# Two-layer graph kernel on one core: last row group in two pairs, its variance from parts, and y parts as upper halves of float32 words

## Chip, cores, metric

One core of one Trainium2 chip. The metric is device time in microseconds (us) of the whole kernel; the time before is the median of 3 runs.

## What is computed

The input is x (2048 x 64, float32), a 0/1 matrix adj (2048 x 2048, float32, about two ones per row), and the weights of two layers. Cut to what matters:

```python
# layer 0: exponentially weighted neighbours by rank, at most 100 per row
support = x @ w0
mask = (adj != 0); rank = cumsum(mask, axis=1); deg = rank[:, -1:]
k = minimum(deg, 100); pos = rank - (deg - k)
w = mask * where(pos > 0, 0.5 ** (k - pos), 0)
x = layernorm(x + w @ support + b0)              # eps 1e-5, over 64
# layer 1: mean of the neighbours and the row itself, then row-normalised
deg = clip(sum(adj, axis=1) + 1, 1)
h = (adj @ x + x) / deg
z = concatenate([x, h], axis=1) @ W1 + b1
r = relu(z); r = r / maximum(norm(r, axis=1), 1e-12)
out = layernorm(x + r)
```

## The kernel before, in words

Rows are cut into 16 tiles of 128 partitions, and four tiles make a group (0 to 3). The order of work on each engine is written out by hand: every engine has its own program, in order, and semaphores tie them. The adjacency matrix comes in 1 MB pieces, TensorE transposes it (`transpose_adj`, L648; it reads the upper bf16 halves of the float32 words as stationary operand) into `adjT`, VectorE copies it out of PSUM (L484), and for each tile of columns TensorE counts ranks (`count`, L662 and L664, into PSUM `cnt`), ScalarE turns the counts into bf16 weights (`weights`, L296), and TensorE multiplies them with the support (`weigh`, L675, into `acc`). A count waits for the weights of the count before it in its chain. Chain 0 (groups 0 and 2) and chain 1 (groups 1 and 3, five ticks behind) alternate in one loop of 37 ticks (L742 to L770).

VectorE finishes layer 0 of each group (`finish_layer0`, L405 to L439), giving `x1`. TensorE transposes it (`transpose_x1`, L685) and multiplies with W1 (`multiply_x1`, L694) to y and u. y is kept as three bf16 parts in `ysp` beside a column of ones: ScalarE rounds the first part (`y_high`, L307), VectorE subtracts (L431), ScalarE rounds the second (`y_middle`, L312), VectorE subtracts again for the third (L438, semaphore `y_ready`). `aggregate` (L706) multiplies the transposed adjacency (with the identity added, L248 on GpSimd) with these 193 columns, 16 source blocks for each of 16 row tiles, 256 matmuls; they are called in portions as blocks become ready: `early` is blocks 0 to 7, `third` 8 to 11, `fourth` 12 to 15 (L739 to L741, L765 to L797). Group 0 sums in the lower half of `acc`, group 1 in the two `cnt` banks, group 2 in the upper half of `acc`, group 3 in `tmp`. Semaphore `agg_done` counts finished groups.

Behind it stands the end of the kernel, for each group k of four tiles. VectorE: `clip` (degree, L503), `total` (sum of the three parts, L506), `limit` (L511). ScalarE: `weigh_u` (u times degree, four activations, L346). VectorE: `add_u` (L517). ScalarE: `relu` (L351). VectorE: `norm_stats` (two batch-norm statistics, L388), `mean_square` (L527), `add_spread` (L532), `clamp` (L538). GpSimd: `norm_power` (power -0.5, L252). Then r is centred and scaled: for groups 0 and 1 by VectorE's `shift_mean` (L543) and four ScalarE activations (`shift_scale`, L356), for groups 2 and 3 on VectorE (`centre` L548, `scale` L554). VectorE: `add_x1` (L559), `spread_stats` (L388 again). GpSimd: `spread_power` (multiply and add, L256, then power -0.5, L259). VectorE: `output` (L568). SyncE stores each group (L216), in the order 1, 0, 2, 3. The list of calls that sets VectorE's order stands in L571 to L620, GpSimd's in L262 to L269, ScalarE's in L359 to L368. VectorE's own dependencies go through the semaphore `chain` (`done`, `need`).

Of the kernel before, what the change touches and what calls it, by code (L numbers as in the profile page):

```python
# [33 lines left out]
STORES = (1, 0, 2, 3)  # L34
# [9 lines left out]
def build(nc, x, adj, w0, b0, w1, b1, out):  # L44
    with ExitStack() as ctx:  # L45
# [22 lines left out]
        ysp = sb("ysp", [P, NB, PD + 2], BF16)  # L68
# [11 lines left out]
        stats = sb("stats", [P, 2, NB, 3], F32)  # L80
# [3 lines left out]
        shift = sb("shift", [P, NB], F32)  # L84
        power = sb("power", [P, RT], F32)
        eps = sb("eps", [P, 1], F32)
        root = sb("root", [P, 2, NB], F32)
        small = sb("small", [P, 4, NB], F32)
# [40 lines left out]
        y_mid = sem("y_mid")  # L129
# [4 lines left out]
        degree_ready = [sem(f"degree_ready{k}") for k in range(Q)]  # L134
        weighted = [sem(f"weighted{k}") for k in range(Q)]
        z_ready = [sem(f"z_ready{k}") for k in range(Q)]
        relued = [sem(f"relued{k}") for k in range(Q)]
        clamped = [sem(f"clamped{k}") for k in range(Q)]
        norm_root = [sem(f"norm_root{k}") for k in range(Q)]
        shift_ready = [sem(f"shift_ready{k}") for k in range(Q)]  # L140
        scaled = [sem(f"scaled{k}") for k in range(Q)]
        spread_ready = [sem(f"spread_ready{k}") for k in range(Q)]
        spread_root = [sem(f"spread_root{k}") for k in range(Q)]
        power_set = sem("power_set")
        variance = [sem(f"variance{k}") for k in range(Q)]
        out_ready = [sem(f"out_ready{k}") for k in range(Q)]
# [26 lines left out]
        def step(q, b):  # L173
            return (q // 2) * NB + NB - 1 - b

# [10 lines left out]
        def _(sp):  # L186
# [27 lines left out]
            for k in STORES:  # L214
                sp.wait_ge(out_ready[k], 1)
                sp.dma_start(out_v[:, rows(k), :], outs[:, rows(k), :]).then_inc(stored, 16)  # L216
            sp.wait_ge(stored, 16 * Q)

        @block.gpsimd
        def _(pool):  # L220
# [29 lines left out]
            def norm_power(k):  # L250
                pool.wait_ge(clamped[k], 1)
                nc.gpsimd.tensor_tensor(small[:, 3, rows(k)], square[:, rows(k)], power[:, :], ALU.pow).then_inc(norm_root[k], 1)  # L252

            def spread_power(k):
                pool.wait_ge(spread_ready[k], 2)
                nc.gpsimd.tensor_scalar(small[:, 0, rows(k)], stats[:, 0, rows(k), 2], 1.0 / D, LN_EPS, ALU.mult,  # L256
                                        ALU.add).then_inc(variance[k], 1)
                pool.wait_ge(variance[k], 1)
                nc.gpsimd.tensor_tensor(small[:, 1, rows(k)], small[:, 0, rows(k)], power[:, :],  # L259
                                        ALU.pow).then_inc(spread_root[k], 1)  # L260
# [11 lines left out]
        def _(act):  # L272
# [37 lines left out]
            def y_middle(q):  # L310
                act.wait_ge(y_left, q + 1)
                nc.scalar.copy(ysp[:, rows(q), D:2 * D], left32[:, rows(q), :]).then_inc(y_mid, 1)  # L312

            for tick in range(TICKS):
# [8 lines left out]
                for q in range(2):  # L323
                    if tick == ENDS[q] + 2:
                        spread_root0(q)
                    if tick == ENDS[q] + 3:
                        copy_x1T(q)
                    if tick == ENDS[q] + 4:
                        y_high(q)
                    if tick == ENDS[q] + 5:  # L330
                        y_middle(q)
# [6 lines left out]
            y_middle(2)  # L338
            copy_x1T(3)
            y_high(3)  # L340
            y_middle(3)

            def weigh_u(k):
                act.wait_ge(degree_ready[k], 1)
                for t in range(k * RT, k * RT + RT):
                    nc.scalar.activation(u1[:, t, :], u1[:, t, :], ACT.Copy,  # L346
                                         scale=degree[:, t:t + 1]).then_inc(weighted[k], 1)

            def relu(k):
                act.wait_ge(z_ready[k], 1)  # L350
                nc.scalar.activation(t1[:, rows(k), :], t0[:, rows(k), :], ACT.Relu).then_inc(relued[k], 1)  # L351

            def shift_scale(k):
                act.wait_ge(shift_ready[k], 1)
                for t in range(k * RT, k * RT + RT):
                    nc.scalar.activation(t2[:, t, :], t1[:, t, :], ACT.Identity, bias=shift[:, t:t + 1],  # L356
                                         scale=small[:, 3, t:t + 1]).then_inc(scaled[k], 1)

            weigh_u(0)  # L359
            relu(0)  # L360
            weigh_u(1)
# [3 lines left out]
            shift_scale(0)  # L365
            shift_scale(1)
            weigh_u(3)
            relu(3)  # L368
        @block.vector
        def _(dve):  # L370
# [15 lines left out]
            def measure(k, q, data):  # L386
                for t in range(q * RT, q * RT + RT, 2):
# [3 lines left out]
            def inverse_root(k, q, i):  # L391
                v = rows(q)
                y, h = small[:, 2 * k, v], small[:, 2 * k + 1, v]
                if i == 1:
                    return nc.vector.reciprocal(y, root[:, k, v])
                if i == 2:
                    return nc.vector.scalar_tensor_tensor(out=h, in0=y, scalar=-4.0 / D if k == 0 else -4.0, in1=y,
                                                          op0=ALU.mult, op1=ALU.mult)
                if i == 3:
                    return nc.vector.scalar_tensor_tensor(out=h, in0=stats[:, 0, v, 2] if k == 0 else square[:, v],  # L400
                                                          scalar=D * LN_EPS if k == 0 else 0.0, in1=h,
                                                          op0=ALU.add, op1=ALU.mult)
                return nc.vector.scalar_tensor_tensor(out=h, in0=h, scalar=3.0, in1=y, op0=ALU.add, op1=ALU.mult)

            def finish_layer0(q, part):  # L405
# [9 lines left out]
                if part == 2:  # L415
                    for stat in measure(0, q, t0):
# [5 lines left out]
                if part == 4:  # L422
                    dve.wait_ge(rooted, q + 1)
                    for i in range(1, 5):
                        link(inverse_root(0, q, i))
# [74 lines left out]

            def clip(k):
                dve.wait_ge(agg_done, k + 1)
                nc.vector.tensor_scalar(degree[:, rows(k)], agg[k][:, :, PD], 1.0, None, ALU.max).then_inc(degree_ready[k], 1)  # L503

            def total(k):
                done(nc.vector.reduce_sum(t0[:, rows(k), :],  # L506
                                          agg[k][:, :, 0:PD].rearrange("p t (k d) -> p t d k", k=PARTS), AX_X), k, "total")

            def limit(k):
                dve.wait_ge(degree_ready[k], 1)  # L510
                done(nc.vector.scalar_tensor_tensor(out=bound[:, rows(k)], in0=degree[:, rows(k)], scalar=SS_MIN,  # L511
                                                    in1=degree[:, rows(k)], op0=ALU.mult, op1=ALU.mult), k, "limit")

            def add_u(k):
                need(k, "total")
                dve.wait_ge(weighted[k], RT)
                nc.vector.tensor_tensor(t0[:, rows(k), :], t0[:, rows(k), :], u1[:, rows(k), :],  # L517
                                        ALU.add).then_inc(z_ready[k], 1)

            def norm_stats(k):  # L520
                dve.wait_ge(relued[k], 1)
                for stat in measure(1, k, t1):
                    done(stat, k, "norm_stats")

            def mean_square(k):
                need(k, "norm_stats")
                done(nc.vector.scalar_tensor_tensor(out=square[:, rows(k)], in0=stats[:, 1, rows(k), 1], scalar=float(D),  # L527
                                                    in1=stats[:, 1, rows(k), 1], op0=ALU.mult, op1=ALU.mult), k, "mean_square")

            def add_spread(k):  # L530
                need(k, "mean_square")
                done(nc.vector.tensor_tensor(square[:, rows(k)], square[:, rows(k)], stats[:, 1, rows(k), 2], ALU.add),  # L532
                     k, "add_spread")

            def clamp(k):
                need(k, "add_spread")
                need(k, "limit")
                nc.vector.tensor_tensor(square[:, rows(k)], square[:, rows(k)], bound[:, rows(k)],  # L538
                                        ALU.max).then_inc(clamped[k], 1)

            def shift_mean(k):
                dve.wait_ge(norm_root[k], 1)
                nc.vector.scalar_tensor_tensor(out=shift[:, rows(k)], in0=stats[:, 1, rows(k), 1], scalar=-1.0,  # L543
                                               in1=small[:, 3, rows(k)], op0=ALU.mult, op1=ALU.mult).then_inc(shift_ready[k], 1)

            def centre(k):
                need(k, "norm_stats")
                done(nc.vector.scalar_tensor_tensor(out=t1[:, rows(k), :], in0=spread(stats[:, 1, rows(k), 1]), scalar=-1.0,  # L548
                                                    in1=t1[:, rows(k), :], op0=ALU.mult, op1=ALU.add), k, "centre")

            def scale(k):
                need(k, "centre")
                dve.wait_ge(norm_root[k], 1)
                nc.vector.tensor_tensor(t2[:, rows(k), :], t1[:, rows(k), :], spread(small[:, 3, rows(k)]),  # L554
                                        ALU.mult).then_inc(scaled[k], RT)

            def add_x1(k):
                dve.wait_ge(scaled[k], RT)
                done(nc.vector.tensor_tensor(t0[:, rows(k), :], t2[:, rows(k), :], x1[:, rows(k), :], ALU.add), k, "add_x1")  # L559
# [263 lines left out]
```

## Time and profile before

| what | value |
|---|---|
| median of 3 runs | 120.68 us (119.8 to 120.87) |
| the profiled execution | 118.94 us |
| its span, first to last instruction | 117.2 us |
| mean granted TensorE clock | 0.948 of 2.4 GHz |
| TensorE matmul / weight load busy | 96.1 / 78.1 us |
| VectorE / ScalarE / GpSimd busy | 60.1 / 55.9 / 18.6 us |

All durations below are those of the one profiled execution; its time is 1.74 us above its span. Its time is also 1.74 us below the median of the runs. Busy times are modelled for pipelined matmuls: their starts are exact, their ends overlap.

### The profile page before, as it was taken

How to read it: one execution, taken by the hardware profiler on the slowest of the kernel's cores; microseconds unless marked ns; L12 is line 12 of the kernel's file. 1: busy time of each engine (PE TensorE's matmuls, PEld its weight loads, DVE VectorE, ACT ScalarE, POOL GpSimd, SP SyncE). 2: the span in 40 equal slices, each digit the busy share in tenths (PEclk: the TensorE clock that was granted, in tenths of full speed). 3: DMA queues.
4: the chain of work that ended last, by engine and by line, in shares of the span. 5: the costliest groups of instructions: out<-in, count | busy, mean ns of one | idle time of the engine just before them, and what ended most of it. 6: DMA issues, size and time to landing. Idle time of an engine off the chain costs nothing.

```text
span 117.2 us, 2438 instructions
## 1 busy us (share of the span) xinstructions
PE 96.1 (82%) x929; PEld 78.1 (67%) x940; DVE 60.1 (51%) x153; ACT 55.9 (48%) x115; POOL 18.6 (16%) x44
## 2 busy tenths in 40 slices
PE   0394799999999999999999999979999999980000
PEld 0292488877777777776777777749989999970000
DVE  1026036465334377636575523472592268869831
ACT  0605435477666565666575756443132155774000
POOL 6200000000000522000540000000000002471790
PEclk9999779999999999999999999999999999999555
DMA  3999999999999999910000000000000000000033
GB/s 75 316 290 338 386 386 387 391 384 291 391 385 386 389 386 386 348 64 0 0 8 0 0 6 0 0 0 6 0 0 0 6 0 0 0 6 0 0 90 89
DMA packets 13978, 18.14 MB, mean 155 GB/s; under 512 B 5264, under 2 KB 6288, under 8 KB 13968
## 3 DMA queue, kind: packets, MB, share of 16 engines
q1 hardware_dynamic: 13808, 17.96, 44.2%
q8 instruction: 8, 0.13, 0.4%
q10 hardware_dynamic: 160, 0.03, 0.1%
q14 instruction: 2, 0.02, 0.0%
HBM read 17.47 MB, written 0.52 MB: 153 GB/s over the span
## 4 chain that ended last, share of the span: by engine, by line
PE 75%; DVE 6%; issue 4%; POOL 4%; DMA 3%; ACT 3%; POOLq 1%; SPq 1%
PE acc L675 16%; PE cnt L664 12%; PE tmp L648 12%; PE acc L706 9%; PE cnt L662 9%; PE tmp L706 5%; PE cnt L706 5%; DMA stage<-in_adj_dram 3%; PE tmp L694 3%; POOL small L259 2%; PE acc L720 2%; ACT wts L296 2%; DVE adjT L484 1%; POOL small L256 1%; POOLq L45 1%
## 5 line engine op out<-in xcount | busy, mean ns | idle before, releaser
L296 ACT ACTIVATE wts<-cnt 128x512 int16<-128x512 f32 x64 | 37.8, 597 | 27.4 <-PE cnt L664 26.8
L484 DVE COPY adjT<-tmp 128x1024 bf16<-128x1024 bf16 x32 | 22.1, 689 | 28.2 <-PE tmp L648 28.2
L675 PEld LDWEIGHTS acc<-sup,wts 128*128 128x128 bf16 x256 | 23.2, 99 | 13.8 <-issue 0.5
L675 PE MATMUL acc<-sup,wts 128*128 128x192 bf16 x256 | 31.4, 248 | 0.1
L664 PE MATMUL cnt<-adjT,suffix 128*128 128x512 bf16 x63 | 24.6, 390 | 0.7 <-ACT wts L296 0.3
L648 PE MATMUL tmp<-ident,stage 128*128 128x128 bf16 x256 | 20.9, 229 | 1.3 <-DMA stage<-in_adj_dram 0.9
L662 PE MATMUL cnt<-adjT,rest 128*128 128x512 bf16 x50 | 19.2, 384 | 2.8 <-ACT wts L296 2.7
L648 PEld LDWEIGHTS tmp<-ident,stage 128*128 128x128 bf16 x256 | 17.8, 103 | 3.0 <-issue 2.6
L248 POOL TENSOR_TENSOR adjT<-adjT,ident 128x128 bf16<-128x128 bf16 x16 | 6.3, 427 | 51.8 <-PE cnt L664 51.8
L706 PE MATMUL acc<-ysp,adjT 128*128 128x193 bf16 x128 | 12.0, 247 | 0.0
L706 PEld LDWEIGHTS acc<-ysp,adjT 128*128 128x128 bf16 x128 | 11.0, 98 | 0.2
L252 POOL TENSOR_TENSOR small<-square,power 128x4 f32<-128x4 f32 x4 | 4.3, 1070 | 42.3 <-DVE square L538 42.3
L662 PEld LDWEIGHTS cnt<-adjT,rest 128*128 128x128 bf16 x60 | 5.9, 98 | 4.5 <-ACT wts L296 3.4
L664 PEld LDWEIGHTS cnt<-adjT,suffix 128*128 128x128 bf16 x64 | 6.3, 99 | 0.4
L346 ACT ACTIVATE u<-u,degree 128x64 f32<-128x64 f32 x16 | 4.3, 336 | 4.8 <-DVE degree L503 4.8
L388 DVE BATCH_NORM_STATS2 stats<-t 128x6 f32<-128x128 f32 x24 | 5.8, 286 | 1.3 <-ACT t L351 1.2
L706 PE MATMUL cnt<-ysp,adjT 128*128 128x193 bf16 x64 | 5.9, 247 | 0.0
L706 PEld LDWEIGHTS cnt<-ysp,adjT 128*128 128x128 bf16 x64 | 5.5, 97 | 0.2
L706 PE MATMUL tmp<-ysp,adjT 128*128 128x193 bf16 x64 | 5.6, 246 | 0.0
L706 PEld LDWEIGHTS tmp<-ysp,adjT 128*128 128x128 bf16 x64 | 5.5, 97 | 0.0
L411 DVE TENSOR_REDUCE t<-acc 128x256 f32<-128x768 f32 x4 | 3.8, 958 | 2.5 <-PE acc L675 2.4
L431 DVE TENSOR_TENSOR left<-tmp,ysp 128x256 f32<-128x256 f32 x4 | 1.7, 422 | 5.5 <-ACT ysp L307 4.3
(76 smaller groups left out, 72.3 us busy)
## 6 DMA issues: line engine op xcount, KB each, us to landing
stage<-in_adj_dram SPq DMA_DIRECT2D x15, 1024.0 KB, 12.3
stage<-in_adj_dram SPq DMA_DIRECT2D x4, 256.0 KB, 4.0
xs<-in_x_dram SPq DMA_DIRECT2D x2, 256.0 KB, 5.7
out_dram<-outs SPq DMA_DIRECT2D x4, 128.0 KB, 1.9
wd<-in_L_gnn_W_dram SPq DMA_DIRECT2D x4, 16.0 KB, 8.5
wd<-in_L_gnn_weight_dram ACTq DMA_DIRECT2D x2, 16.0 KB, 3.7
b0row<-in_L_gnn_bias_dram SPq DMA_DIRECT2D x1, 32.0 KB, 11.2
b1row<-in_L_gnn_b_dram SPq DMA_DIRECT2D x1, 32.0 KB, 9.0
```

The costliest lines, as they stand in the source:

```text
L248: nc.gpsimd.tensor_tensor(d, d, ident16[:, :], ALU.add).then_inc(diag_ready, 1)
L252: nc.gpsimd.tensor_tensor(small[:, 3, rows(k)], square[:, rows(k)], power[:, :], ALU.pow).then_inc(norm_root[k], 1)
L296: nc.scalar.activation(wts[:, c, n % WRING, :].bitcast(I16), cnt[:, c, :], ACT.Relu).then_inc(w_ready[c], 1)
L346: nc.scalar.activation(u1[:, t, :], u1[:, t, :], ACT.Copy, scale=degree[:, t:t + 1]).then_inc(weighted[k], 1)
L388: yield nc.vector.bn_stats(stats[:, k, t:t + 2, :].rearrange("p s c -> p (s c)"), data[:, t:t + 2, :].rearrange("p t d -> p d t"))
L411: nc.vector.reduce_sum(t0[:, v, :], sums, AX_X).then_inc(acc_read, 1)
L484: nc.vector.tensor_copy(adjT[:, 2 * bp:2 * bp + 2, q * CH:(q + 1) * CH], bank.bitcast(BF16).rearrange("p (k n) -> p k n", k=2)).then_inc(t ...
L648: last = nc.tensor.transpose(bank[:, k * CH + r * P:k * CH + (r + 1) * P], halves[:, r, 2 * j0 + 1:2 * (j0 + P):2], ident16[:, :])
L662: nc.tensor.matmul(cnt[:, c, :], rest[:, :], adjT[:, b + 1, i0:i0 + CH], start=False, stop=False, skip_group_check=True)
L664: nc.tensor.matmul(cnt[:, c, :], suffix[:, :], adjT[:, b, i0:i0 + CH], start=(b == NB - 1), stop=True, skip_group_check=True).then_inc(cnt ...
L675: last = nc.tensor.matmul(acc[:, c * RT + r, 0:PD], wts[:, c, n % WRING, r * P:(r + 1) * P], sup[:, b, :], start=(b == NB - 1 and r % 2 == ...
L706: last = nc.tensor.matmul(agg[g][:, r, 0:PD + 1], adjT[:, b, t * P:(t + 1) * P], ysp[:, b, 0:PD + 1], start=first, stop=(b == NB - 1), ski ...
```

## The change

Three things are changed. (a) `ysp` is float32 instead of bf16. The y parts are written as float32, and TensorE, and VectorE where it subtracts, read the upper bf16 half of each word; `y_middle` on ScalarE is gone. (b) The aggregation is reordered: two portions of group 1 (8 matmuls each) go into ticks 33 and 34 of the loop, and group 3 is aggregated as two pairs of tiles, each with its own count of `agg_done`. (c) The end works on five batches (groups 0 to 2, tiles 12-13, tiles 14-15). `output` of batches 0 and 1 moves to ScalarE, batch 0's scaling moves from ScalarE to VectorE, batch 3's from VectorE to ScalarE. Batch 4 doesn't use GpSimd: its inverse roots are made of a ScalarE square root and a VectorE reciprocal with one correction step, and its variance is put together from the variance of x1, of r, and their product's sum, without waiting for x1 + r.

```diff
-STORES = (1, 0, 2, 3)
+BATCHES = ((0, 4), (4, 8), (8, 12), (12, 14), (14, 16))
+LAST = (4,)
+STORES = (0, 1, 2, 4, 3)
...
-        ysp = sb("ysp", [P, NB, PD + 2], BF16)
+        ysp = sb("ysp", [P, NB, PD + 2], F32)
...
+        def top(a):
+            return a.bitcast(BF16)[:, :, 1::2]
...
             norm_power(0)
             norm_power(1)
+            spread_power(0)
             norm_power(2)
-            spread_power(0)
+            spread_power(1)
             norm_power(3)
-            spread_power(1)
             spread_power(2)
             spread_power(3)
...
-            def y_middle(q):
-                act.wait_ge(y_left, q + 1)
-                nc.scalar.copy(ysp[:, rows(q), D:2 * D], left32[:, rows(q), :]).then_inc(y_mid, 1)
...
+            def output(k):
+                act.wait_ge(root_ready[k], 1)
+                for t in range(*BATCHES[k]):
+                    nc.scalar.activation(outs[:, t, :], t0[:, t, :], ACT.Copy,
+                                         scale=small[:, 1, t:t + 1]).then_inc(out_ready[k], 1)
+
+            def norm_root(k):
+                act.wait_ge(clamped[k], 1)
+                nc.scalar.activation(root[:, 1, batch(k)], square[:, batch(k)], ACT.Sqrt).then_inc(root_ready[k], 1)
+
+            def spread_root(k):
+                act.wait_ge(variance_ready[k], 1)
+                nc.scalar.activation(root[:, 0, batch(k)], small[:, 0, batch(k)], ACT.Sqrt).then_inc(root_ready[k], 1)
+
             weigh_u(0)
+            weigh_u(1)
             relu(0)
-            weigh_u(1)
             relu(1)
             weigh_u(2)
             relu(2)
-            shift_scale(0)
             shift_scale(1)
             weigh_u(3)
+            output(0)
             relu(3)
+            weigh_u(4)
+            relu(4)
+            output(1)
+            norm_root(4)
+            shift_scale(3)
+            shift_scale(4)
+            spread_root(4)
...
-                    nc.vector.tensor_tensor(left32[:, v, :], bank[:, :, 0, :], ysp[:, v, 0:D],
+                    nc.vector.tensor_tensor(ysp[:, v, D:2 * D], bank[:, :, 0, :], top(ysp[:, v, 0:D]),
                                             ALU.subtract).then_inc(y_left, 1)
...
-                    dve.wait_ge(y_mid, q + 1)
-                    nc.vector.tensor_tensor(ysp[:, v, 2 * D:3 * D], left32[:, v, :], ysp[:, v, D:2 * D],
+                    dve.wait_ge(y_left, q + 1)
+                    nc.vector.tensor_tensor(ysp[:, v, 2 * D:3 * D], ysp[:, v, D:2 * D], top(ysp[:, v, D:2 * D]),
                                             ALU.subtract).then_inc(y_ready, 1)
...
-                                                ysp[:, b, 0:PD + 1], start=first, stop=(b == NB - 1),
+                                                ysp[:, b, 0:PD + 1].bitcast(BF16)[:, 1::2], start=first, stop=(b == NB - 1),
...
+                if STEPS < tick < STEPS + LAG:
+                    pe.wait_ge(y_ready, 2)
+                    pe.wait_ge(diag_ready, PT)
+                    pe.wait_ge(w_ready[0], STEPS)
+                    aggregate(1, early, [tick - STEPS - 1])
...
             transpose_x1(2)
-            aggregate(1, early, range(0, 2))
+            aggregate(1, early, [2])
             multiply_x1(2)
-            aggregate(1, early, range(2, RT))
+            aggregate(1, early, [3])
+            pe.wait_ge(acc_read, 4)
+            aggregate(2, early, [0, 1])
             transpose_x1(3)
-            pe.wait_ge(acc_read, 4)
-            aggregate(2, early, range(0, 2))
+            aggregate(2, early, [2])
             multiply_x1(3)
             pe.wait_ge(y_ready, 3)
             aggregate(0, third)
-            aggregate(2, early, range(2, RT))
+            aggregate(1, third)
             pe.wait_ge(y_ready, 4)
             aggregate(0, fourth).then_inc(agg_done, 1)
-            aggregate(1, third)
             aggregate(1, fourth).then_inc(agg_done, 1)
+            aggregate(2, early, [3])
             aggregate(2, third)
             aggregate(2, fourth).then_inc(agg_done, 1)
             read(("x1T", 3))
             read(("yu", 3))
-            aggregate(3, early)
-            aggregate(3, third)
-            aggregate(3, fourth).then_inc(agg_done, 1)
+            aggregate(3, range(NB), range(0, 2)).then_inc(agg_done, 1)
+            aggregate(3, range(NB), range(2, RT)).then_inc(agg_done, 1)
```

The new end of VectorE's list (before it, batches 0 to 2 follow the old pattern, with batches 0 and 1 side by side), calls in one line where they follow each other:

```text
... scale(0) add_u(2) add_x1(0) shift_mean(1) limit(2) spread_stats(0) total(3) clip(3) norm_stats(2) limit(3)
mean_square(2) add_x1(1) add_spread(2) add_u(3) clamp(2) spread_stats(1) centre(2) clip(4) total(4) limit(4)
norm_stats(3) add_u(4) mean_square(3) scale(2) add_spread(3) norm_stats(4) clamp(3) mean_square(4) add_x1(2)
add_spread(4) product(4) clamp(4) spread_stats(2) shift_mean(3) norm_recip(4) norm_half(4) norm_first(4)
norm_error(4) covariance(4) norm_inverse(4) share(4) shift_mean(4) add_x1(3) fixed(4) cross(4) spread_stats(3)
variance(4) output(2) spread_recip(4) spread_half(4) spread_first(4) spread_error(4) add_x1(4)
spread_inverse(4) output(4) output(3)
```

`product` multiplies r and x1 (128 x 128), `covariance` sums that over 64 columns; all other new calls of batch 4 are one instruction on 128 x 2 numbers each. Ahead of `clip(0)`, one statistic of x1 (tiles 14, 15) and one small instruction are added.

## Rows read from the trace of the kernel before

**Rows 1.** The page: TensorE's busy time, its granted clock, engines of the last chain.

```profile
PE 96.1 (82%) x929; PEld 78.1 (67%) x940; DVE 60.1 (51%) x153; ACT 55.9 (48%) x115; POOL 18.6 (16%) x44
...
PEclk9999779999999999999999999999999999999555
...
PE 75%; DVE 6%; issue 4%; POOL 4%; DMA 3%; ACT 3%; POOLq 1%; SPq 1%
```

**Rows 2.** Chain that ended last, from 90 us on (start us, us, what).

```profile
90.02 4.09 PE acc L706 x48
...
99.56 5.46 PE tmp L706 x64
...
108.78 1.01 POOL small L252
...
111.81 1.06 POOL small L259
...
114.51 0.42 DVE outs L568
```

**Rows 3.** The same chain, at ticks 33 to 35 of the loop.

```profile
75.93 0.66 PE acc L675 x8
76.59 0.26 issue
76.85 0.39 PE cnt L664
...
77.27 0.60 ACT wts L296
77.87 0.24 issue
78.11 0.38 PE cnt L662
```

**Rows 4.** Timeline of the end (start us, us, engine, line, operation, out<-in, count).

```profile
91.43 0.42 DVE L438 TENSOR_TENSOR ysp<-left,ysp 128x256 bf16<-128x256 f32 x1
...
105.98 0.15 DVE L511 SCALAR_TENSOR_TENSOR bound<-degree 128x4 f32<-128x4 f32 x1
106.05 0.42 DVE L554 TENSOR_TENSOR t<-t,small 128x256 f32<-128x256 f32 x1
...
107.93 0.16 DVE L527 SCALAR_TENSOR_TENSOR square<-stats 128x4 f32<-128x4 f32 x1
108.13 0.16 DVE L532 TENSOR_TENSOR square<-square,stats 128x4 f32<-128x4 f32 x1
...
110.15 1.06 POOL L259 TENSOR_TENSOR small<-small,power 128x4 f32<-128x4 f32 x1
110.38 0.42 DVE L559 TENSOR_TENSOR t<-t,x 128x256 f32<-128x256 f32 x1
...
111.25 0.76 DVE L568 TENSOR_TENSOR outs<-t,small 128x256 f32<-128x256 f32 x2
111.30 0.43 POOL L256 TENSOR_SCALAR small<-stats 128x4 f32<-128x4 f32 x1
111.70 3.63 SPq L216 DMA_DIRECT2D out_dram<-outs  x4
```

**Rows 5.** Groups by line and shape, 75 to 118 us (busy us, mean ns | idle before).

```profile
L346 ACT ACTIVATE u<-u,degree 128x64 f32<-128x64 f32 x16 | 4.3, 336 | 4.8 <-DVE degree L503 4.8
L356 ACT ACTIVATE t<-t,shift,small 128x64 f32<-128x64 f32 x8 | 2.9, 427 | 0.1
L388 DVE BATCH_NORM_STATS2 stats<-t 128x6 f32<-128x128 f32 x20 | 4.8, 287 | 1.3 <-ACT t L351 1.2
L694 PE MATMUL tmp<-wd,x1T 128*128 128x256 f32 x8 | 2.1, 386 | 0.0
L506 DVE TENSOR_REDUCE t<-tmp 128x256 f32<-128x768 f32 x1 | 0.9, 947 | 0.0
L312 ACT CAST ysp<-left 128x256 bf16<-128x256 f32 x2 | 0.8, 405 | 1.8 <-DVE left L431 1.8
L289 ACT ACTIVATE root<-stats,eps 128x4 f32<-128x4 f32 x2 | 0.6, 294 | 1.4 <-DVE stats L388 1.4
```

More of the change, by code:

```diff
@@ L499, in need, with sums, own_spread @@
                 dve.wait_ge(chain, made[k, name])
+            def sums(k):
+                g, r = BATCHES[k][0] // RT, BATCHES[k][0] % RT
+                return agg[g][:, r:r + size(k), :]
+            def own_spread(k):
+                for t in range(BATCHES[k][0], BATCHES[k][1], 2):
+                    done(nc.vector.bn_stats(stats[:, 2, t:t + 2, :].rearrange("p s c -> p (s c)"),
+                                            x1[:, t:t + 2, :].rearrange("p t d -> p d t")), k, "own_stats")
+                need(k, "own_stats")
+                done(nc.vector.tensor_scalar(own[:, batch(k)], stats[:, 2, batch(k), 2], 1.0 / D, LN_EPS, ALU.mult,
+                                             ALU.add), k, "own_spread")
@@ L501, in clip @@
             def clip(k):
                 dve.wait_ge(agg_done, k + 1)
[L503 removed]
+                nc.vector.tensor_scalar(degree[:, batch(k)], sums(k)[:, :, PD], 1.0, None, ALU.max).then_inc(degree_ready[k], 1)
             def total(k):
[L506 to L507 removed]
+                dve.wait_ge(agg_done, k + 1)
@@ L564, in spread_stats @@
                     stat.then_inc(spread_ready[k], 1)
             def output(k):
-                dve.wait_ge(spread_root[k], 1)
-                nc.vector.tensor_tensor(outs[:, rows(k), :], t0[:, rows(k), :], spread(small[:, 1, rows(k)]),
-                                        ALU.mult).then_inc(out_ready[k], 1)
+                need(k, "add_x1")
+                if k in LAST:
+                    need(k, "spread_inverse")
+                else:
+                    dve.wait_ge(root_ready[k], 1)
@@ new lines, in output, with product, covariance @@
+                nc.vector.tensor_tensor(outs[:, batch(k), :], t0[:, batch(k), :], spread(small[:, 1, batch(k)]),
+                                        ALU.mult).then_inc(out_ready[k], size(k))
+            def product(k):
+                dve.wait_ge(relued[k], 1)
+                done(nc.vector.tensor_tensor(t3[:, 0:size(k), :], t1[:, batch(k), :], x1[:, batch(k), :], ALU.mult), k, "product")
+            def covariance(k):
+                need(k, "product")
+                done(nc.vector.reduce_sum(small[:, 4, batch(k)], t3[:, 0:size(k), :], AX_X), k, "covariance")
@@ new lines, in norm_recip, with share, fixed @@
+            def norm_recip(k):
+                dve.wait_ge(clamped[k], 1)
+                done(nc.vector.reciprocal(small[:, 5, batch(k)], square[:, batch(k)]), k, "norm_recip")
+            def share(k):
+                need(k, "norm_recip")
+                done(nc.vector.scalar_tensor_tensor(out=small[:, 6, batch(k)], in0=stats[:, 1, batch(k), 2], scalar=1.0 / D,
+                                                    in1=small[:, 5, batch(k)], op0=ALU.mult, op1=ALU.mult), k, "share")
+            def fixed(k):
+                need(k, "share")
+                need(k, "own_spread")
+                done(nc.vector.tensor_tensor(small[:, 6, batch(k)], small[:, 6, batch(k)], own[:, batch(k)], ALU.add),
+                     k, "fixed")
@@ new lines, in norm_first, with norm_half @@
+            def norm_first(k):
+                dve.wait_ge(root_ready[k], 1)
+                need(k, "norm_recip")
+                done(nc.vector.tensor_tensor(small[:, 7, batch(k)], root[:, 1, batch(k)], small[:, 5, batch(k)], ALU.mult),
+                     k, "norm_first")
+            def norm_half(k):
+                dve.wait_ge(root_ready[k], 1)
+                done(nc.vector.scalar_tensor_tensor(out=small[:, 8, batch(k)], in0=root[:, 1, batch(k)], scalar=-0.5,
+                                                    in1=root[:, 1, batch(k)], op0=ALU.mult, op1=ALU.mult), k, "norm_half")
@@ new lines, in cross, with variance @@
+            def cross(k):
+                need(k, "norm_inverse")
+                need(k, "covariance")
+                done(nc.vector.scalar_tensor_tensor(out=small[:, 4, batch(k)], in0=small[:, 4, batch(k)], scalar=2.0 / D,
+                                                    in1=small[:, 3, batch(k)], op0=ALU.mult, op1=ALU.mult), k, "cross")
+            def variance(k):
+                need(k, "cross")
+                need(k, "fixed")
+                nc.vector.tensor_tensor(small[:, 0, batch(k)], small[:, 4, batch(k)], small[:, 6, batch(k)],
+                                        ALU.add).then_inc(variance_ready[k], 1)
@@ L571, in _ @@
+            for k in LAST:
+                own_spread(k)
             clip(0)
@@ L585, in _ @@
             total(2)
-            mean_square(1)
-            add_spread(1)
+            scale(0)
             add_u(2)
-            clamp(1)
+            add_x1(0)
+            shift_mean(1)
             limit(2)
-            shift_mean(0)
+            spread_stats(0)
+            total(3)
+            clip(3)
             norm_stats(2)
+            limit(3)
             mean_square(2)
+            add_x1(1)
             add_spread(2)
+            add_u(3)
+            clamp(2)
+            spread_stats(1)
@@ L595, in _ @@
             centre(2)
-            clamp(2)
-            shift_mean(1)
-            add_x1(0)
-            spread_stats(0)
-            clip(3)
-            total(3)
-            limit(3)
+            clip(4)
+            total(4)
+            limit(4)
+            norm_stats(3)
+            add_u(4)
+            mean_square(3)
             scale(2)
-            add_u(3)
+            add_spread(3)
+            norm_stats(4)
+            clamp(3)
+            mean_square(4)
             add_x1(2)
-            add_x1(1)
@@ L607, in _ @@
-            norm_stats(3)
-            mean_square(3)
-            add_spread(3)
-            centre(3)
-            clamp(3)
-            spread_stats(1)
-            spread_stats(2)
-            scale(3)
+            add_spread(4)
+            product(4)
+            clamp(4)
+            spread_stats(2)
+            shift_mean(3)
+            norm_recip(4)
+            norm_half(4)
+            norm_first(4)
+            norm_error(4)
+            covariance(4)
+            norm_inverse(4)
+            share(4)
@@ L615, in _ @@
+            shift_mean(4)
             add_x1(3)
+            fixed(4)
+            cross(4)
             spread_stats(3)
-            output(1)
-            output(0)
+            variance(4)
             output(2)
+            spread_recip(4)
+            spread_half(4)
+            spread_first(4)
+            spread_error(4)
+            add_x1(4)
+            spread_inverse(4)
+            output(4)
             output(3)
```

193 lines of the change are left out of this document (116 added, 77 removed).

## The prediction

> **What bounds the kernel now.** I read the page first. TensorE's matmuls are busy 96.1 of 117.2 us, its granted clock is full (9s, the 2.4 GHz level) until its work ends and half afterwards, and 75% of the chain that ended last is TensorE [rows 1]. So two things can shorten the kernel: idle time of TensorE, and the piece behind its last matmul. Next I read the end of the chain [rows 2]: group 3's 64 matmuls end at 99.56 + 5.46 = 105.02, and the last VectorE instruction ends at 114.51 + 0.42 = 114.93. These 9.9 us are bound first by the VectorE and ScalarE steps of group 3, and from 108.78 by GpSimd, which runs without a real pause from there until VectorE's last instruction begins: one power for group 3's norm, then a sum and a power for each of groups 1, 2 and 3. A power takes 1.01 to 1.06. From 114.93 to the end of the span are 2.27 us, the last store. The third view is the same chain at ticks 33 to 35 [rows 3]: count, ScalarE's weights, count is a loop of 78.11 - 76.85 = 1.26 us, and TensorE has only half a count (0.22) and one `weigh` (0.33, half of the x8 piece) to do in it: 0.71 us idle. One turn earlier there is a further 0.2 of the same kind, part of the 0.26 of "issue".
>
> **(a) y parts as float32 words.** It removes `y_middle`, four ScalarE instructions of 0.405 [rows 5], and a ScalarE step between the two subtractions. The last third part is ready at 91.43 + 0.42 = 91.85 [rows 4], and TensorE asks for it behind two thirds of the x48 piece, at 90.02 + 2.73 = 92.75 [rows 2]: 0.9 of cover, so I count nothing; bounds are 0 and a gain of 0.1. The four freed places lie in ScalarE's idle time. Reading the upper halves costs VectorE nothing in the sum (one element per lane as before). The open cost is TensorE reading its moving operand at every second bf16. No row shows that. The bounds: 0, as the aggregation's pitch now is 5.46 / 64 = 85.3 ns for 193 columns [rows 2], 0.44 ns per column; and twice that, because the float32 product at L694 [rows 5], the nearest row whose moving operand has four-byte words, needs more than one pass over its columns and can't be held to one column in the same time. Twice would be 256 x 85.3 ns = 21.8 us. I take 0: the words are neighbours, and the stationary operand is already read in this way at L648 without a place in the chain of its own.
> The Trainium skill, page "SBUF — State Buffer", section "SBUF: two separate sides" and the box on cachelines under it, says that accesses within one 16-byte line run at full bandwidth and that bf16 may be strided by up to eight elements. By that the cost is 0; no run here shows it yet.
>
> **(b) Aggregation order.** 16 matmuls of group 1 go between the turns of the loop. Followed through from 75.77: `weigh`, portion of 8 (0.68), `weigh`, count at 77.11 instead of 76.63; `weigh`, portion, next count at 78.55 instead of 78.11; from there TensorE never waits and stands 0.44 late, but 16 x 0.085 = 1.36 of later work is done. Net 0.92 of idle time gone; bounds 0 (if the y of group 1 or the accumulator came late; both are ready some 3 us before) and 0.92. The other portions keep each wait covered: 8 matmuls (0.68) stand where 16 stood in front of each `multiply_x1`, against a ScalarE copy of as many numbers as L312's (0.405 [rows 5]) plus its hops, so at most 0.1 is given back. The last matmul ends at 105.02 - 0.9 = 104.1, the first pair of group 3 (32 matmuls, 2.73 earlier) at 101.4, groups 0 to 2 at 93.9, 95.3, 98.7.
>
> **(c) The end.** I keep a ledger: each instruction takes the duration of its row, and starts when the one before it on its engine lets it and its inputs are there. From [rows 4]: an instruction that depends on the one before starts 0.04 after its end (107.93 + 0.16, then 108.13), an independent one 0.08 before its end (105.98 to 106.05). From [rows 4, 5]: 256 numbers 0.42, a statistic 0.287, 768 summed numbers 0.947, so 1.03 ns per number; for pairs that gives the estimates 0.29 for 128 numbers and 0.55 for `total`. ScalarE: 0.336 and each further one 0.24 later (L346), 0.43 and 0.33 later with a bias (L356), a square root on few numbers 0.294 (L289). Hops I take at 0.03 to ScalarE, 0.12 back. GpSimd: sum 0.19 alone, 0.43 beside a VectorE instruction with two inputs (at 111.30, where it ends as L568's first does [rows 4]), power 1.01 to 1.26. For two numbers I keep the price of four; down to half is possible. Laid over the order before, this ledger ends at 114.3 to 115.4, by how GpSimd's gaps are set; the trace says 114.93.
> Over the new order: VectorE has 81 instructions instead of 58 behind the first `agg_done`, and from 99 on it is nearly without a gap. `total(4)` starts at 104.4, 0.3 after the matmuls, behind `centre(2)` and `clip(4)`; add_u(4) ends 105.6, relu 106.0, statistic 106.4, clamp(3) 106.4, clamp(4) 107.2, ScalarE's square root 107.6. `shift_mean(3)` stands in front of batch 4's inverse root and waits for GpSimd's power of batch 3 until 107.75; what is queued behind it is all of batch 4. Then six small instructions and `covariance` (0.8): norm_inverse ends 108.6, `shift_mean(4)` 108.85, two scalings on ScalarE until 109.55, beside which the variance is ready at 109.55. Square root 109.95, four small ones and `add_x1(4)`, spread_inverse 110.7, `output(4)` 111.05, `output(3)` 111.4. GpSimd comes out at the same time: norm(3) to 107.75, sum and power of batch 2 to 109.1, the statistic of batch 3 only at 109.5, sum and power to 111.1. On ScalarE, `output(0)` waits for GpSimd until 103.2 and holds relu(3) and both of batch 4's; relu(3) ends 104.5, its reader is at 104.9, so the cover is 0.4. `output(1)` (1.06 long) ends just when the square root is asked for: cover 0, price at most its 0.3 if it slips. The two instructions on x1 ahead of `clip(0)` fall into VectorE's wait for group 0. On SyncE an issue is 0.37 to 0.5, and batch 4's is out of the way when output(3) ends; a fifth store costs 0, at worst 0.3.
> So the end goes from 114.93 to 111.4, -3.5, of which 0.7 hangs on (b): with the matmuls 0.9 later the ledger ends 0.7 later. Against the profiled execution: 118.94 - 3.5 = 115.4. That execution is 1.74 under the median; from the median of 120.68 the forecast is 117.2.
>
> **Rivals.**
> B: VectorE becomes the bound and is denser than my pitches. If each of the 62 instructions from `clip(2)` on cost 0.04 more, 2.5 us, about a third is covered by waits: 118.8 (118.1 to 119.7). For: no stretch before has so many small ones in a row. Against: the pitches are from its busiest stretch.
> C: GpSimd and VectorE shut each other out wholly. Then from norm(2) on, each of five powers and three sums holds a two-input VectorE instruction for its length: 5 x 1.01 + 3 x 0.19 = 5.6, less 0.9 of waits that the ledger has: +4.7, so 120.68 - 3.5 + 4.7 = 121.9, slower. It decides from 3.5, three powers and a half. Against: L559 with two inputs starts at 110.38, 0.22 after a power started that runs until 111.21, and takes its usual 0.42 [rows 4]. For: GpSimd's sum at 111.30 was held until VectorE ended.
> The same page of the Trainium skill, section "Who interferes with whom", states this rule (two SBUF inputs against a GpSimd instruction that reads SBUF; whoever issues first keeps the pair for the whole instruction). The trace agrees in one direction only.
> D: The strided moving operand costs. At twice the pitch +21.8: about 139, slower; the gain is gone from 3.5 / 256 = 14 ns per matmul, 85 to 99 ns. Against: the reasons under (a).
> E: The change doesn't bring what it says: GpSimd stays the last link. `shift_mean(3)` and output(3) still hang on its powers; were each held as the one of 1.26 is, and batch 3's statistic late by another microsecond behind ScalarE's scalings, the end is near 114: 119.9, no change.
>
> **How the numbers follow.** Forecast 0.68 (own range 116.1 to 118.2, from pitches, half-price powers, the ledger's 0.5 of misfit and the runs' own spread), B 0.16, E 0.07, C 0.05, D 0.04. A measurement of this kernel tells about 1% from no change. Faster by over 1% (below 119.47): 0.68 + 0.14 of B + 0.01 of E = 0.83. Within 1%: 0.08. Slower: 0.09. The range, 115.8 to 119.4, leaves out C, D, nearly all of E and a bit of B.
>
> **What would show it.** In the changed profile: matmuls of L706's successor at 85 ns; the counts of ticks 34 and 35 without the 0.7 idle; last matmul near 104.1; VectorE over 85% busy from 99 to 111 (B if it passes 112 with GpSimd waiting for it); shift_mean(3) waiting for GpSimd; no VectorE instruction starting only when a power ends without needing it (C); last output near 111.4, and output(3) last. Wrong it would be with a pitch over 99 ns, or the last output after 113.7.

## The result, and the profile after

The changed kernel's four runs have a median of 115.82 us (114.96 to 116.86) beside 120.24 (119.25 to 120.87) for the kernel before: ratio 0.962, 95% interval 0.951 to 0.972. The ratio leaves out the changed kernel's slowest run, 116.86, which is over 1.5% above its fastest; the other three have a median of 115.75, just under the lower end of the forecast range, 115.8. Two later comparisons on the chip, with more runs, gave the unchanged copy of the changed kernel 0.984 (0.978 to 0.990) and 0.973 (0.968 to 0.979). The direction was right, and the three measured gains are 3.8%, 1.6% and 2.7%; much of their scatter comes from the first 20 us of the kernel, as the last section shows.

The profiled execution took 114.96 us, span 113.2. First the page: TensorE's busy time and clock, and the last chain by engine.

```profile
PE 95.5 (84%) x929; PEld 78.1 (69%) x940; DVE 61.1 (54%) x178; ACT 57.1 (50%) x122; POOL 17.8 (16%) x44
...
PEclk9999999999999999999999999999999999999755
...
PE 77%; DVE 8%; DMA 4%; issue 3%; ACT 3%; SPq 1%; DVEq 0%
```

Against [rows 1], GpSimd is gone from the chain, and the two slices from 11.7 to 17.6 us, in which the clock before stood at 7, are 9 here. The second difference is no part of the change. Next the chain at ticks 33 to 35 and from the last matmuls on, the views of [rows 3] and [rows 2]:

```profile
75.18 0.33 PE acc L831 x4
75.51 0.71 PE cnt L862 x8
76.22 0.33 PE acc L831 x4
76.60 0.38 PE cnt L820
76.98 0.33 PE acc L831 x4
77.31 0.71 PE cnt L862 x8
78.02 0.22 PE cnt L818
...
98.48 5.67 PE tmp L862 x64
104.17 0.16 DVE degree L534
104.33 0.47 DVE t L538
...
108.18 0.16 DVE small L657
```

The two portions (x8) stand where 0.26 us of issue and the wait for ScalarE's weights stood. But a portion lasts 0.71 and not 0.68: 5.67 / 64 = 88.6 ns from one matmul's start to the next (the pitch), where it was 85.3. The end, in the timeline:

```profile
104.25 0.55 DVE L538 TENSOR_REDUCE t<-tmp 128x128 f32<-128x384 f32 x1
...
106.17 0.95 POOL L263 TENSOR_TENSOR small<-square,power 128x2 f32<-128x2 f32 x1 [0.43 <-DVE square L570]
...
106.94 0.20 ACT L371 ACTIVATE root<-square 128x2 f32<-128x2 f32 x1
107.22 0.16 DVE L579 SCALAR_TENSOR_TENSOR small<-stats,small 128x2 f32<-128x2 f32 x1
...
107.74 0.28 DVE L620 TENSOR_REDUCE small<-t 128x2 f32<-128x128 f32 x1
108.18 0.16 DVE L657 SCALAR_TENSOR_TENSOR small<-small 128x2 f32<-128x2 f32 x1 [0.16 <-DVE small L620]
...
109.24 0.35 POOL L268 TENSOR_SCALAR small<-stats 128x2 f32<-128x2 f32 x1 [0.54 <-DVE stats L414]
109.32 0.19 ACT L375 ACTIVATE root<-small 128x2 f32<-128x2 f32 x1
...
109.68 0.69 POOL L271 TENSOR_TENSOR small<-small,power 128x2 f32<-128x2 f32 x1
...
110.40 0.49 DVE L611 TENSOR_TENSOR outs<-t,small 128x128 f32<-128x128 f32 x2
```

To see it by stages I cut each profile at two marks that all kernels have: the start of the last transpose of the adjacency in the loop (74.89 before, 74.14 after) and the end of the last matmul. Everything in us; each value is a difference of starts and ends in the timelines.

| stage | before | after | change |
|---|---|---|---|
| start to first transpose | 5.99 | 6.41 | +0.42 |
| first to last transpose | 68.90 | 67.73 | -1.17 |
| last transpose to last matmul's end | 30.11 | 29.99 | -0.12 |
| that to the last output's end | 9.93 | 6.76 | -3.17 |
| that to the end of the span | 2.27 | 2.31 | +0.04 |

So 0.75 us of the 4.0 between the two spans came about ahead of anything that the change moves. The change itself is worth 3.3 in this pair. TensorE's stage gained almost nothing, although 0.9 was to come from it, and the end gave more than the 2.6 that the ledger had for it.

### The profile page after: what moved, and what is told of

The parts are those of the page before. It is cut to its first block, busy times and chain, and to the rows that moved or that the text cites. A ratio compares the mean times of both kernels' runs of the same rounds, so it can differ in the third digit from the quotient of the medians.

```text
span 113.2 us, 2490 instructions
## 1 busy us (share of the span) xinstructions
PE 95.5 (84%) x929; PEld 78.1 (69%) x940; DVE 61.1 (54%) x178; ACT 57.1 (50%) x122; POOL 17.8 (16%) x44
## 4 chain that ended last, share of the span: by engine, by line
PE 77%; DVE 8%; DMA 4%; issue 3%; ACT 3%; SPq 1%; DVEq 0%
PE acc L831 17%; PE cnt L820 13%; PE tmp L804 12%; PE acc L862 10%; PE cnt L818 9%; PE tmp L862 5%; PE cnt L862 5%; DMA stage<-in_adj_dram 4%; PE tmp L850 3%; PE acc L876 2%; ACT wts L308 2%; DVE adjT L503 1%; PE tmp L876 1%; DVE x L445 1%; DVE left L467 1%
## 5 line engine op out<-in xcount | busy, mean ns | idle before, releaser
L820 PE MATMUL cnt<-adjT,suffix 128*128 128x512 bf16 x63 | 24.1, 383 | 0.6
L804 PE MATMUL tmp<-ident,stage 128*128 128x128 bf16 x256 | 20.4, 225 | 1.9 <-DMA stage<-in_adj_dram 1.6
L804 PEld LDWEIGHTS tmp<-ident,stage 128*128 128x128 bf16 x256 | 17.1, 101 | 3.5 <-issue 3.0
L862 PE MATMUL acc<-ysp,adjT 128*128 128x193 bf16 x128 | 12.8, 250 | 0.0
L263 POOL TENSOR_TENSOR small<-square,power 128x4 f32<-128x4 f32 (+1 forms) x4 | 4.2, 1055 | 38.3 <-DVE square L570 38.3
L862 PE MATMUL cnt<-ysp,adjT 128*128 128x193 bf16 x64 | 6.6, 250 | 0.0
L450 DVE TENSOR_TENSOR ysp<-tmp,ysp 128x256 f32<-128x256 f32 x4 | 1.7, 423 | 5.1 <-ACT ysp L319 3.9
```

Source lines behind the costliest of these rows:

```text
L263: nc.gpsimd.tensor_tensor(small[:, 3, batch(k)], square[:, batch(k)], power[:, 0:size(k)], ALU.pow).then_inc(norm_ready[k], 1)
L804: last = nc.tensor.transpose(bank[:, k * CH + r * P:k * CH + (r + 1) * P], halves[:, r, 2 * j0 + 1:2 * (j0 + P):2], ident16[:, :])
L820: nc.tensor.matmul(cnt[:, c, :], suffix[:, :], adjT[:, b, i0:i0 + CH], start=(b == NB - 1), stop=True, skip_group_check=True).then_inc(cnt ...
L862: last = nc.tensor.matmul(agg[g][:, r, 0:PD + 1], adjT[:, b, t * P:(t + 1) * P], ysp[:, b, 0:PD + 1].bitcast(BF16)[:, 1::2], start=first, ...
```

## The experiments

All were run beside the kernel before. The stages below are from their profiles; each kernel's first two stages scatter, the others repeat to 0.02 us between profiles of one kernel (the copies of the changed kernel: 30.00 and 6.77, 29.98 and 6.76).

| kernel | last transpose to last matmul | to last output | both | ratio to before |
|---|---|---|---|---|
| before | 30.11 | 9.93 | 40.04 | 1 |
| changed | 29.99 | 6.76 | 36.75 | 0.962, 0.984, 0.973 |
| only_a | 30.87 | 9.93 | 40.80 | 1.019 (1.011 to 1.027) |
| no_a | 29.36 | 6.81 | 36.17 | 0.969 (0.962 to 0.977) |
| no_a_2 | 29.36 | 6.82 | 36.18 | 0.973 (0.969 to 0.977) |
| no_fill | 30.82 | 6.77 | 37.59 | 0.988 (0.979 to 0.998) |
| only_c | 29.99 | 6.83 | 36.82 | 0.972 (0.967 to 0.976) |
| no_last | 29.99 | 7.74 | 37.73 | 0.982 (0.972 to 0.992) |

**Undoing (a), and (a) alone.** `no_a` puts these back into the changed kernel, `only_a` takes them out of the kernel before:

```diff
-        ysp = sb("ysp", [P, NB, PD + 2], F32)
+        ysp = sb("ysp", [P, NB, PD + 2], BF16)
...
+            def y_middle(q):
+                act.wait_ge(y_left, q + 1)
+                nc.scalar.copy(ysp[:, rows(q), D:2 * D], left32[:, rows(q), :]).then_inc(y_mid, 1)
...
-                                                ysp[:, b, 0:PD + 1].bitcast(BF16)[:, 1::2], start=first, stop=(b == NB - 1),
+                                                ysp[:, b, 0:PD + 1], start=first, stop=(b == NB - 1),
```

> The changed kernel with part (a) undone: y parts as bf16 again, with ScalarE's y_middle. Theory 1 (the strided moving operand costs TensorE 88.6 - 85.3 = 3.3 ns a matmul): aggregation pitch back to 85.3 ns, last matmul 0.7 to 0.9 us nearer to the loop's end, and 0.4 to 0.8 us less time than the changed kernel, so about 0.955 of before. Theory 2 (the pitch is no matter of the operand, or (a) itself won the 0.75 us by which the changed profile was ahead at 50 us): pitch stays at 88 to 89 ns, or the time is 0.5 us or more above the changed kernel.

> The kernel before with part (a) alone. Theory 1: pitch 88.6 ns, last matmul 0.8 us later, time 0.5 to 0.9 us above before (ratio 1.004 to 1.008). Theory 2: the same or faster than before.

The aggregation's matmuls in the groups by line and shape (behind the bar: busy us, mean ns of one), first `no_a`'s, then `only_a`'s:

```profile
L871 PE MATMUL acc<-ysp,adjT 128*128 128x193 bf16 x128 | 12.4, 247 | 0.0
L871 PE MATMUL tmp<-ysp,adjT 128*128 128x193 bf16 x64 | 5.6, 247 | 0.0
```

```profile
L701 PE MATMUL acc<-ysp,adjT 128*128 128x193 bf16 x128 | 12.5, 250 | 0.0
L701 PE MATMUL tmp<-ysp,adjT 128*128 128x193 bf16 x64 | 5.8, 250 | 0.0
```

The duration of one matmul (longer than the pitch, because they overlap) is 247 ns with packed parts and 250 with halves, in both surroundings, and the 64 last matmuls take 5.68 in `only_a` against 5.46. TensorE's stage is 0.76 longer with (a) alone, and 0.63 shorter where it is undone. All 256 matmuls at 3.3 ns more make 0.84; the 0.76 leaves at most 0.08 that removing the ScalarE step from the y chain can have won. The 0.63 is smaller because the slower portions also cover more of ScalarE's copies: in the changed kernel `multiply_x1` takes 0.95 twice, in `no_a` 0.97 and 1.05, and the second pair of x1 transposes 0.26 for 0.34, together 0.20. Theory 1 holds.

The ratio of `only_a`, 1.9% above, is more than 0.76 us explain. Its runs fall into two kinds by their mean granted clock, probably the classes of the last section. The four at 0.962 to 0.964 have a mean of 122.09 us, beside 121.44 for the four of the kernel before at 0.966; the two at 0.944 have 120.65, beside 119.74 for its six at 0.946 to 0.950. Like beside like, `only_a` is 0.65 and 0.91 slower, which agrees with 0.76.

**The fillers of (b).** `no_fill`, and `only_c`, which has (a) undone too:

```diff
-                if STEPS < tick < STEPS + LAG:
-                    pe.wait_ge(y_ready, 2)
-                    pe.wait_ge(diag_ready, PT)
-                    pe.wait_ge(w_ready[0], STEPS)
-                    aggregate(1, early, [tick - STEPS - 1])
...
-            aggregate(1, early, [2])
+            aggregate(1, early, [0, 1, 2])
```

> The changed kernel without the two portions in ticks 33 and 34 (they stand behind transpose_x1(2) again). Theory 1: 0.9 us of TensorE's idle time is back, the last matmul is 0.9 us later, and the time is 0.6 to 0.9 above the changed kernel. Rival: VectorE, dense from 99 us on, is the bound of the end, so the loss is 0.3 us or less.

> Parts (a) and (b)'s fillers both undone: packed bf16 parts, and the two portions of ticks 33 and 34 behind transpose_x1(2) again; pairs and the new end stay. If the parts add up: 36.2 + 0.8 = 37.0 us from the last transpose to the last output, 6.8 of it behind the last matmul, and a ratio about 0.975 of before. Rival: without the filler the end, which hangs on VectorE, hides part of the loss, 36.5 or less.

The chain of `no_fill` in that stretch:

```profile
77.49 0.23 PE cnt L820
77.72 0.02 issue
77.74 0.61 ACT wts L308
78.35 0.24 issue
78.59 0.38 PE cnt L818
```

The wait of [rows 3] is back. TensorE's stage grows by 0.83 beside halves, and by 0.63 beside packed parts; the last output comes later by as much (37.59 - 36.75 = 0.84, 36.82 - 36.17 = 0.65). So the end does not hide it: although VectorE is busy 11.22 of the 12 us from 99 to 111 in the changed kernel, its list waits for the last `agg_done`. And 36.82 against an expected 37.0 says that the parts add up to within 0.2.

**How the last pair is finished.** `no_last` keeps the pairs and treats the last as the others:

```diff
-LAST = (4,)
-STORES = (0, 1, 2, 4, 3)
+LAST = ()
+STORES = (0, 1, 2, 3, 4)
...
             norm_power(3)
+            norm_power(4)
             spread_power(2)
             spread_power(3)
+            spread_power(4)
...
-            norm_root(4)
-            spread_root(4)
```

> The changed kernel with its two pairs, but the last pair treated as the others: its inverse roots by GpSimd's powers, its variance from statistics of x1 + r. The parts (covariance, own variance, reciprocal and correction) are left out, outputs in the order 2, 3, 4. From the last matmul to the last output the changed kernel takes 6.77 us and the kernel before 9.93. Theory 1: GpSimd is a serial chain again, norm(3), norm(4), and a sum and a power for each of batches 2, 3 and 4; about 0.95 + 0.95 + 1.3 + 1.0 + 1.0 from norm(3)'s start, so 7.5 to 7.9 us. Rival 1: the split into pairs alone brings it all, 6.8. Rival 2: the batch without GpSimd brings it all, above 9.

Its timeline:

```profile
107.05 1.60 POOL L263 TENSOR_TENSOR small<-square,power 128x2 f32<-128x2 f32 x2 [0.43 <-DVE square L570]
...
109.02 1.01 POOL L271 TENSOR_TENSOR small<-small,power 128x4 f32<-128x4 f32 x1
...
110.38 0.90 POOL L271 TENSOR_TENSOR small<-small,power 128x2 f32<-128x2 f32 x1
111.36 0.19 POOL L268 TENSOR_SCALAR small<-stats 128x2 f32<-128x2 f32 x1
...
111.64 0.69 POOL L271 TENSOR_TENSOR small<-small,power 128x2 f32<-128x2 f32 x1
112.46 0.29 DVE L611 TENSOR_TENSOR outs<-t,small 128x128 f32<-128x128 f32 x1 [0.76 <-POOL small L271]
```

GpSimd is the serial chain again, and the stage is 7.74. So of the 3.17 won at the end, 0.97 comes from taking the last pair off GpSimd, its variance from parts included, and 2.2 from the rest: the pairs of (b), and of (c) the new orders and the outputs on ScalarE. These 2.2 were not split further.

**What the strided operand costs by size.** `stride4` puts ysp's words two apart; `wide_bf16` and `wide_f32` use 256 columns. To make room, some tiles of these three share memory with others that are no longer in use.

```diff
-                                                ysp[:, b, 0:PD + 1].bitcast(BF16)[:, 1::2], start=first, stop=(b == NB - 1),
+                                                ysp[:, b, 0:YS * (PD + 1)].bitcast(BF16)[:, 1::2 * YS], start=first, stop=(b == NB - 1),
```

> Packed bf16 parts (part (a) undone), with 256 columns of ysp in each aggregation matmul instead of 193; the added 63 columns are ones and are not read afterwards. Pitch about 85.3 + 63 x 0.42 = 112 ns in every theory. It is the measure for wide_f32.

> The same 256 columns, as upper halves of float32 words. Theory 1a, the strided operand costs a fixed time per matmul: 3.3 ns above wide_bf16. Theory 1b, it costs per column: 3.3 x 256 / 193 = 4.4 ns above.

> The changed kernel with the float32 words of ysp two apart, so that TensorE reads one bf16 in every eight bytes instead of four. If the extra time of 3.3 ns is a matter of the stride in bytes it grows, to about 6 to 10 ns above 85.3 (or to twice the pitch, if a threshold is passed); if it is the same for every operand that isn't packed, the pitch stays at 88.6.

The last 64 matmuls in the chains of `wide_bf16`, `wide_f32` and `stride4`:

```profile
103.47 7.00 PE tmp L871 x64
```

```profile
103.85 7.27 PE tmp L862 x64
```

```profile
117.56 11.14 PE tmp L866 x64
```

| bytes from one bf16 to the next | columns | ns per matmul |
|---|---|---|
| 2 | 193 | 85.3 |
| 4 | 193 | 88.6 |
| 2 | 256 | 109.4 |
| 4 | 256 | 113.6 |
| 8 | 193 | 174.1 |

Four bytes cost 3.3 ns on 193 columns and 4.2 on 256, so it goes by the column (4.4 expected), about 4%. Eight bytes cost the double: `stride4` took 140.03 us in its one run. I had expected 92 to 95 ns, or the double if a threshold is passed; the double it is. Half the clock would double the pitch as well, but the chain of `stride4` has other matmuls right beside a portion, and they take what they took before (0.22 and 0.33):

```profile
82.23 0.22 PE cnt L822
82.45 0.22 PE cnt L824
82.67 0.33 PE acc L835 x4
83.00 1.39 PE acc L866 x8
```

Where between four and eight bytes the price jumps was not tried, nor why it does. The three kernels of this table with other strides or widths ran once each; their pitches are from one profile each.

**The changed kernel and its packed version again.**

> The changed kernel itself, as a measure beside the others: ratio 0.955 to 0.97 of before.

> The changed kernel with packed bf16 parts once more, in one call with the changed kernel. Theory: from the last transpose of the adjacency to the last output 36.2 us against 36.8, and 0.4 to 0.8 us less time than the changed kernel where their fronts (up to the loop's steady part) are alike. Rival: the gain is within what the fronts scatter, and the times are the same.

> The changed kernel itself beside it: 36.8 us in that stretch, ratio to before between 0.96 and 0.985.

By stages the packed version is 0.60 and 0.56 us better (36.17 against 36.77, and 36.18 against 36.74). In time it can't be told: beside each other the ratios were 0.969 and 0.984 the first time, which is more than 0.6 us explain, and 0.9729 and 0.9731 the second. So the times bear out the rival of `no_a_2`, that the gain is lost in the scatter of the fronts, and only the stages bear out its theory.

## Why the prediction was right or wrong

**Idle time of TensorE (b): right in kind, 0.2 too large.** Predicted 0.92 net; with packed parts TensorE's stage went from 30.11 to 29.36, 0.75. The step that was mis-sized is "at most 0.1 is given back". The chain of `no_a` has `multiply_x1` twice:

```profile
85.17 0.97 PE tmp L859 x4
...
89.21 1.05 PE tmp L859 x4
```

Both pieces took 0.89 before: 8 matmuls don't quite cover ScalarE's copy. These 0.24, less 0.07 by which the second pair of x1 transposes got shorter (0.34 for 0.41), are the missing 0.17.

**Strided operand (a): wrong.** "I take 0" was the step. It is 3.3 ns per matmul, 0.63 to 0.76 in the stage, and ate what (b) won. Rival D had the mechanism with too high a price for this stride; at twice the stride its price is there, to within 4%. My reason that the stationary operand is read in this way already said nothing of the moving one. The Trainium skill, page "SBUF — State Buffer", box on cachelines in section "SBUF: two separate sides", would have bf16 free up to a stride of eight elements, so both strides at no cost; measured are 4% at two elements and 104% at four, and the measurement decides.

**The end (c): right in its steps, 0.6 too small.** The last matmul ended at 104.13, as forecast (104.1), but that was luck: the faster front (-0.75) and the strided operand (+0.6 to 0.8) happened to cancel. `total(4)` started at 104.25 (forecast 104.4), clamp(3) ended at 106.09 (106.4), clamp(4) at 106.90 (107.2). The step that was mis-sized is "For two numbers I keep the price of four", and with it `shift_mean(3)` waiting for GpSimd until 107.75. The power on two numbers took 0.95 beside the two-input L598, where I had 1.26 for that case; it also began 0.3 earlier, and ended at 107.12. VectorE came to `shift_mean(3)` at 107.22, 0.08 before the end of the statistic in front of it, as an instruction does that waits for nothing; no piece of GpSimd's is in the last chain. By this place the whole half microsecond had been won: from there to the last output it was 3.67, forecast 3.65. The last power took 0.69 where I had kept the price of four, 1.01; ScalarE's roots took 0.20 and 0.19 instead of 0.294. GpSimd was done at 110.37, before output(4) began, so output(3) didn't wait for it either; it ended at 110.89, forecast 111.4. "Down to half is possible" named the bound; I took the other end.

**The sum.** -3.5 from one execution; the two stages that the change touches gave -3.29. That is within 0.2, and by two errors of opposite sign: 0.8 missing in TensorE's stage, 0.6 more at the end; that they came so near is luck. From the profiled execution before, 118.94, to that after, 114.96, are 3.98 less; what the stages of the change don't explain is the front's 0.75. The forecast of 117.2 was taken from a median of three runs, 120.68, and 115.75 is 1.45 below it. So what put the measured time under the range is the start of the sum, a median of three runs, together with too small a width for "the runs' own spread": the first two stages, in which the change touches nothing but `y_middle`, end at 74.14 in one profile of the changed kernel and at 76.15 in another. How much of the 1.45 is the front in the executions without a profile is not known. In the two later comparisons the changed kernel's medians were 117.3 and 116.22, inside the range. Neither of the signs named for being wrong appeared: the pitch stayed under 99 ns and the last output came before 113.7.

**The rivals.** B: VectorE was as dense as said, busy 11.22 of the 12 us from 99 on, and most of its starts follow each other as before. A few behind several waits are later than the ledger's 0.04: L657 starts 0.16 behind the end of L620, and output(4) 0.13 behind the instruction that it needs (110.27 to 110.40). But the end behind the last matmul got shorter than forecast instead of longer, so B fell. C fell too: in the timeline after, VectorE's L598 with two inputs in the on-chip memory starts in the middle of a power and takes its usual time.

```profile
101.70 1.01 POOL L271 TENSOR_TENSOR small<-small,power 128x4 f32<-128x4 f32 x1
...
102.48 0.42 DVE L598 TENSOR_TENSOR t<-t,x 128x256 f32<-128x256 f32 x1
```

E fell in part: `no_last` shows that GpSimd is the last link as soon as the last pair goes through it, but that costs 0.97, not 3.

## What to carry to other kernels

Price a strided moving operand by its own run before building on it: here every second bf16 cost 4% of each matmul and every fourth the double, and saving four ScalarE copies that nobody waited for didn't pay for that. Where a slow engine's serial chain ends the kernel, give the last piece of work another path and keep the slow engine for those before it. Compare kernels whose starts scatter by stages between marks that all of them have: here that told 0.6 us apart, where the times of six runs each showed 1.5% once and nothing the second time.

## What was not expected of the hardware

The stretch from the first to the last transpose of the adjacency, where all these kernels do the same work but for `y_middle`, took 67.73 or 67.74 (changed, `no_a`, `no_a_2`), 68.64 to 68.92 (before, `after_again`, `no_fill`, `only_c`, `no_last`) or 70.27 and 70.32 (`after_3`, `only_a`), the same program falling into more than one class. Of the kernels with other widths or strides, 68.88 (`wide_bf16`) and 68.80 (`wide_f32`) belong to the second, and 69.90 (`stride4`) is nearest to the third. The difference arises between 12 and 20 us: there, some executions run count matmuls at half speed for a while. A count of two matmuls in `after_3`, against the changed kernel's own profile at the same work:

```profile
14.71 0.61 PE L818 MATMUL cnt<-adjT,rest 128*128 128x512 bf16 x1
15.11 0.64 PE L820 MATMUL cnt<-adjT,suffix 128*128 128x512 bf16 x1
15.53 0.85 PE L831 MATMUL acc<-sup,wts 128*128 128x192 bf16 x4
```

```profile
14.38 0.39 PE L818 MATMUL cnt<-adjT,rest 128*128 128x512 bf16 x1 [0.24 <-ACT wts L308]
14.61 0.38 PE L820 MATMUL cnt<-adjT,suffix 128*128 128x512 bf16 x1
14.82 0.49 PE L831 MATMUL acc<-sup,wts 128*128 128x192 bf16 x4
```

From start to start they are 0.40 and 0.42 apart against 0.23 and 0.21: the level of 1.2 GHz against that of 2.4. Before these stretches TensorE had idled between its first counts. In the middle class the page's clock row shows a dip there, to between 5 and 8; in `after_3`, `only_a` and `stride4` it shows 9 throughout, as in the fastest class, so the row didn't tell. The mean granted clock is even the highest where the front is slowest: 0.957 to 0.960 in the middle class, 0.969 to 0.974 in the fastest and 0.980 in `after_3`, all kernels with the new end. With the first transpose between 5.88 and 7.82 us, this makes over 2 us of scatter from profile to profile that no part of the change touches. Whether something in a kernel tips the class was not tried; the classes fell on kernels with and without (a), and the changed kernel's three profiles fell into all three.
